# A post-LN decoder layer: who adds the output products behind the last heads, and the order of a top-k search

## The reference, cut to what matters

```python
x = ln(x + attn(x))           # 16 heads of 128; Wq, Wk, Wv, Wo are 4-bit codes times block scales
x = ln(x + xattn(x, ctx))     # ctx 2 x 1024 x 512
x = ln(x + ffn(x))            # silu(x Wg) * (x Wu), then Wd, 2048 inner features

def xattn(x, ctx):
    s = coef * (x @ Wqx.T) @ ctx.T                # [rows, 1024]
    s = s - max(s)
    thr = top_k(s, 54)[..., -1:]                  # the 54 largest of each row stay
    p = softmax(where(s < thr, -inf, s))
    return (p @ ctx) @ Wox.T
```

## Time and profile before

| | |
|---|---|
| Median of 3 runs | 959.24 us (959.2 to 959.57) |
| The profiled execution | 959.11 us, of which its span is 957.3 us |
| Busy, share of the span | TensorE 923.4 us (96%), VectorE 594.9 (62%), ScalarE 581.2 (61%), GpSimd 482.9 (50%) |
| The chain that ended last | TensorE 78%, VectorE 11%, ScalarE 5%, issue 4%, DMA 1% |
| Mean granted TensorE clock | 0.992 |

### The profile page before, as it was taken

How to read it: one execution, slowest core, us unless ns; L and a number is a source line. 1 busy time by engine, 2 the same in 40 slices (tenths; PEclk the granted TensorE clock), 3 DMA queues, 4 the chain that set the end, 5 groups by cost and what they waited for, 6 DMA issues and landing times.

```text
span 957.3 us, 13364 instructions
## 1 busy us (share of the span) xinstructions
PE 923.4 (96%) x4500; PEld 752.7 (79%) x4500; DVE 594.9 (62%) x1066; ACT 581.2 (61%) x1202; POOL 482.9 (50%) x377
## 2 busy tenths in 40 slices
PE   9999999999999999999999999799999899999997
PEld 7787778877788777877767787798878788888885
DVE  5666956578566676567585899984878214521114
ACT  4667876687766778687875456534655634443333
POOL 4256642646516366367664447543674751364440
PEclk9999999999999999999999999989999999999999
DMA  6531220122301222222122212332443241243331
GB/s 199 155 106 49 83 89 1 53 65 72 93 8 29 88 61 71 69 56 78 44 67 89 67 43 89 89 100 59 130 120 97 84 128 45 96 124 93 96 87 44
DMA packets 46103, 76.98 MB, mean 80 GB/s; under 512 B 5584, under 2 KB 11216, under 8 KB 45776
## 3 DMA queue, kind: packets, MB, share of 16 engines
q1 hardware_dynamic: 45600, 75.68, 27.0%
q10 hardware_dynamic: 432, 0.39, 0.1%
HBM read 73.69 MB, written 2.36 MB: 79 GB/s over the span
## 4 chain that ended last, share of the span: by engine, by line
PE 78%; DVE 11%; ACT 5%; issue 4%; DMA 1%; POOL 0%; SPq 0%; ACTq 0%; DVEq 0%; POOLq 0%
PE p L908 6%; PE p L909 6%; PE p L912 6%; PE p L681 5%; PE p L716 5%; PE p L683 4%; PE p L726 3%; PE p L703 3%; PE p L730 3%; PE p L727 3%; PE p L922 3%; PE p L924 3%; PE p L923 3%; PE p L663 2%; PE p L659 2%
## 5 line engine op out<-in xcount | busy, mean ns | idle before, releaser
L1517 DVE TENSOR_SCALAR_CACHE_REDUCE JK<-p,ssc 128x512 bf16<-128x512 f32 x112 | 83.8, 748 | 124.1 <-PE p L663 124.1
L2082 POOL TENSOR_TENSOR acc<-SX,acc 128x512 f32<-128x512 f32 x54 | 69.8, 1293 | 169.7 <-ACT SX L1075 141.9
L1999 POOL TENSOR_TENSOR V<-RAW,V 128x512 fp32r<-128x512 f32 x64 | 82.9, 1318 | 142.8 <-ACT V L1095 142.8
L1037 ACT ACTIVATE PR<-p,nms,ssc 128x512 f32<-128x512 f32 x112 | 87.2, 779 | 57.8 <-DVE JK L1517 56.8
L681 PE MATMUL p<-R 128*128 128x512 f32 x248 | 97.4, 393 | 1.0 <-DVE V L1510 0.8
L1999 POOL TENSOR_TENSOR C<-RAW,C 128x512 fp32r<-128x512 f32 x58 | 76.1, 1325 | 39.4 <-ACT C L1095 39.2
L1834 DVE TENSOR_TENSOR SX<-p,SX 128x512 f32<-128x512 f32 x32 | 22.1, 691 | 115.4 <-PE p L912 108.9
L1530 DVE TENSOR_TENSOR PT<-p,PT 128x512 fp32r<-128x512 f32 x128 | 87.4, 683 | 4.8 <-ACT PT L1060 4.7
L716 PE MATMUL p<-ident,PR 128*128 128x128 f32 x512 | 78.3, 275 | 0.5
L1060 ACT ACTIVATE PT<-p 128x512 fp32r<-128x512 f32 x128 | 75.7, 591 | 0.7 <-PE p L716 0.7
L683 PE MATMUL p<-R 128*128 128x512 f32 x192 | 75.1, 391 | 0.0
(11 more groups left out here) (246 smaller groups left out, 2711.7 us busy)
## 6 DMA issues: line engine op xcount, KB each, us to landing
RAW<-in_wg SPq DMA_DIRECT2D x32, 256.0 KB, 2.8
RAW<-in_wu SPq DMA_DIRECT2D x32, 256.0 KB, 2.7
RAW<-in_ctxn SPq DMA_DIRECT2D x32, 256.0 KB, 2.7
RAW<-in_wd SPq DMA_DIRECT2D x32, 256.0 KB, 2.7
RAW<-in_wq SPq DMA_DIRECT2D x19, 256.0 KB, 2.7
RAW<-in_wk SPq DMA_DIRECT2D x18, 256.0 KB, 2.7
RAW<-in_wv SPq DMA_DIRECT2D x16, 256.0 KB, 2.7
RAW<-in_wo SPq DMA_DIRECT2D x16, 256.0 KB, 4.7
```

Of the source, the lines that this page charges most:

```text
L1037: e.activation(PR[:, i % 2, :], P[i % 2][:, :], ACT.Exp, bias=nms[:, i % 4:i % 4 + 1], scale=ssc[:, 0:1] if HB[j][0] > 1 else SC, accum_ou ...
L1517: e.tensor_scalar(JK[:, :], P[i % 2][:, :], ssc[:, 1:2] if HB[i // 4][0] > 1 else -SC, None, ALU.mult, ALU.min, accum_out=nms[:, i % 4:i % ...
L1999: e.tensor_tensor(lo, RAW[:, slot[key], :], hi, ALU.subtract).then_inc(*c_lo.up(key))
```

## The change

- **Pairs 14 and 15 (and no longer VectorE).** `scaled_by_act` now also holds for n = 56 to 63; n = 54 and 55 stay with VectorE. From n = 54 on the scaled products go to CB and BO, not to SX0. GpSimd's addition becomes `add_scaled`; the four of pair 15 stand behind its loop, ahead of its low halves of `conv_ct(1, 4..7)`. On ScalarE the four `o_scale` of pair 15 alternate with those conversions, ahead of the table load for the square root.
- **The bias row** is made at i = 110 and added at i = 111 to 118, since CB and BO have to be free.
- **VectorE behind the loop**: one search step instead of three, the four first halves, the statistics of rows 4 to 7, then the reciprocal and application of rows 4 and 5, one step, those of rows 6 and 7, and three steps.
- **`alone`**: tiles 2 and 3 are ended by a new list that holds the rest of that tile only; `until` had alternated with tiles 3, 4 and 5.

```diff
+    def alone(self, n):
+        z = n % 2
+        assert self.live[z][0] == n
+        out = [(n, s) for s in range(self.live[z][1], 16)]
+        self.done.add(n)
+        self.live[z] = [n + 2, 0]
+        if n + 2 > 7:
+            del self.live[z]
+        return out
...
-        if i == 114:
+        if i == 110:
             take("borow")
...
-    return h == 1 and (q < 13 or q == 13 and tt < 2)
+    return h == 1 and not (q == 13 and tt >= 2)
...
+        def scaled_at(n):
+            return OBUF[:, n % 2] if n < 54 else (CB, BO)[n % 2][:, :]
...
 # ScalarE, behind the loop
-            for n in range(4, 8):
-                conv_ct(1, n)
-            search(topk.run(3))
+            for tt in range(4):
+                o_scale(NJ // 2 - 1, tt)
+                conv_ct(1, 4 + tt)
             act_table(ACT.Sqrt)
             ln_std(1, 4, 2)
+            search(topk.run(3))
+            ln_std(1, 6, 2)
             search(topk.run(1))
-            ln_std(1, 6, 2)
...
-            search(topk.until(2))
+            search(topk.alone(2))
             for hf in range(2):
                 px_high(2, hf, 6 + hf)
             conv_cn()
-            search(topk.until(3))
+            search(topk.alone(3))
             for hf in range(2):
                 px_high(3, hf, 6 + hf)
...
 # VectorE, behind the loop
             ot_low(NJ - 1)
-            search(topk.run(3))
+            search(topk.run(1))
             for tt in range(4):
                 o_add(NJ // 2 - 1, tt, 0)
-                o_add(NJ // 2 - 1, tt, 1)
-                if tt == 1:
-                    ln_stats(1, [4, 5], (15, 1))
-                    ln_rstd(1, 4, 2)
-                elif tt == 2:
-                    ln_apply(1, 4, 4)
-                    ln_apply(1, 5, 4)
+            ln_stats(1, [4, 5], (15, 1))
             ln_stats(1, [6, 7], (15, 1))
+            ln_rstd(1, 4, 2)
+            ln_apply(1, 4, 4)
+            ln_apply(1, 5, 4)
             search(topk.run(1))
             ln_rstd(1, 6, 2)
             ln_apply(1, 6, 6)
             ln_apply(1, 7, 6)
-            search(topk.run(1))
+            search(topk.run(3))
...
             cross_add(1, 5)
-            search(topk.until(2))
-            search(topk.until(3))
+            search(topk.alone(2))
+            search(topk.alone(3))
...
 # GpSimd
-                if 115 <= i <= 122:
-                    add_bias(i - 115, "bo2")
+                if 111 <= i <= 118:
+                    add_bias((4, 0, 1, 2, 3, 5, 6, 7)[i - 111], "bo2")
...
+            for tt in range(4):
+                add_scaled(NJ // 2 - 1, tt)
             for n in range(4, 8):
                 conv_ct(1, n)
```

More of the change, by code:

```diff
@@ L263, in row_writers @@
     out = ["bo1"] + [(q, h) for q in qs for h in range(2)]
-    if b == 0 and tt < 2:
-        out += [(12, 0), (12, 1), (13, 0), (13, 1), "bo2"]
-    elif b == 0:
+    if b == 0:
         out += [(12, 0), (12, 1), "bo2", (13, 0), (13, 1)]
@@ L1074, in o_scale @@
                     w.wait_ge(*masked_in[a].at())
-                e.activation(OBUF[:, n % 2], P[BANK["o", q, tt, 1]][:, :], ACT.Copy,
+                if n >= 54:
+                    w.wait_ge(*borowp.at())
+                    w.wait_ge(*rows[7].at("bo2"))
+                e.activation(scaled_at(n), P[BANK["o", q, tt, 1]][:, :], ACT.Copy,
                              scale=ri[:, 4 * (j % 4) + tt:4 * (j % 4) + tt + 1]).then_inc(*oscl.up((q, tt)))
@@ L1125, in conv_cn @@
                         w.wait_ge(*borowp.at())
-                        w.wait_ge(*rows[7].at("bo2"))
+                        w.wait_ge(*rows[7].at((15, 1)))
                     elif n < 5:
@@ L1995, in add_bias, with add_scaled @@
                 e.tensor_tensor(acc[:, r], acc[:, r], BO[:, :], ALU.add).then_inc(*rows[r].up(which))
+            def add_scaled(q, tt):
+                r = 4 * HB[2 * q][1] + tt
+                w.wait_ge(*oscl.at((q, tt)))
+                w.wait_ge(*rows[r].before((q, 1)))
+                e.tensor_tensor(acc[:, r], scaled_at(4 * q + tt), acc[:, r], ALU.add).then_inc(*rows[r].up((q, 1)))
             def conv(key, hi, lo):
@@ L2077, in gpsimd @@
                 if o_tile(i) and scaled_by_act(*o_tile(i), 1):
[L2078 to L2083, removed]
+                    add_scaled(*o_tile(i))
                 if i >= 2:
```

## The result

The changed kernel takes **969.1 us** (median of 4 runs, 968.1 to 970.5) where the kernel before, run beside it, takes 959.4 us: ratio 1.0106, 95% interval 1.0088 to 1.0124, so 9.7 us slower (10.2 by the ratio). The forecast was 966.7 us, with a range of 961.0 to 970.5. The profiled execution took 969.74 us, a span of 967.9 us, 10.6 more than that of before (957.3).

What follows compares the result with a forecast made beforehand. TensorE, busy nearly all the time, was taken as the bound, with VectorE's search deciding from 543 to 577 us. Terms +0.6 +1.4 +1.0 +0.7 +3.9 = +7.6 on 959.1 gave 966.7 us, range 961.0 to 970.5.

Steps and rivals of the forecast that it cites:

- bias row: Its product, ScalarE copy and GpSimd additions move four steps earlier: taken as 0 us, bounds -0.6 to +0.6.
- forecast A: Whole kernel, the prediction's main case: 964 to 970.5 us, chance 0.55.
- tile 3: Tiles listed alone, 612 to 623 us: exponential behind four copies and a conversion, +1.0 us, bounds +0.6 to +1.8.
- block 11: Feed-forward: tile 6's exponential comes late and holds its transposes and the output products; +3.9 us with clock, bounds +3.0 to +5.5.
- up to tile 0's exponential: Behind the last head: VectorE sheds additions but GpSimd holds applications; +0.6 us, bounds -2.0 to +1.3.
- half clock behind it: Behind the last head: TensorE's clock halves after idling some 3 us for the fourth query part; +1.4 us, bounds 0 to 2.6.
- blocks 5, 6: Feed-forward: one more exponential ahead of block 6's table load and activation; +0.7 us, bounds +0.6 to +1.2.
- GpSimd holds three of the four applications: VectorE behind the last head: first application free, other three slowed by GpSimd's work, 0.8 us each.
- GpSimd busy beside the mask: Tile 3's stage: GpSimd's work beside VectorE's mask raises the cost from +0.8 to +1.0 us.
- The place of the exponential: ScalarE at tile 3: exponential behind four copies and one conversion, so the product starts at 623.1 instead of 622.34; +0.8 us.
- The geometry: Block 11: output products that stood before TensorE's old wait now stand behind it; +3.4 us without the clock.
- Rival D: Feed-forward step lists keep their old place, so tile 6's transposes are not held: faster, 955.4 us, chance 0.06.

## Why the prediction was right, and where its sizes were off

Forecast +7.6 us, measured +9.7: forecast A, with every term's sign and place right, and a sum two us too small. The two us are mainly two sizes, the mask and half clock at tile 3 and the half clock in block 11.

| term | forecast | in the profile | by experiment |
|---|---|---|---|
| bias row | 0 | 0 | 0.0 at 484.97 |
| up to tile 0's exponential | +0.6 | +0.5 | 2.6 with the clock |
| half clock behind it | +1.4 | +1.1 | |
| tile 3 | +1.0 | +2.2 | 2.35, of it 1.02 the mask |
| blocks 5, 6 | +0.7 | +0.85 | 4.8 with block 11 |
| block 11 | +3.9 | +4.55 | 3.40 + 1.16 of clock |

**Behind the last head.** All steps came as forecast: the 1.93 us gone, an idle of 2.08 us for row 4, tile 0's exponential 0.5 us late, TensorE idle 3.53 us at the fourth query part. The choice on which the term hung, that GpSimd holds three of the four applications, was right: the four took 4.75 us, and 2.00 once GpSimd waits, so they were held for 2.75 us, where three held ones had been priced at some 2.5 from the earlier trace rows. That the first one slipped through was partly luck: with the wait filled, the same instructions took 5.88 us, all four held, and tile 0's exponential came 1.1 us later behind the score copy than in the changed kernel (31.23 and 30.10 us). The half clock behind it is the loose term: 1.1 us in the profile of the changed kernel, but 2.4 in that with joint lists (tile 2's transposes at 618.73, 3.4 late, against 0.95 at the fourth query part). No run takes it out by itself, so its size stays open within these two.

The SBUF — State Buffer page of the Trainium skill, section Who interferes with whom, says that the port pair is an exclusive lock for the length of an instruction, and that an instruction of VectorE with two SBUF inputs meets it when GpSimd reads SBUF. The traces agree in size: a mask that starts 0.03 us behind a conversion of 1.26 us takes 1.03 us more, and a MATCH_REPLACE8, with one such input, none. The applications, TENSOR_SCALAR with one such tensor, are held all the same, so the count of inputs alone does not tell who is.

**Tile 3 is the term that was mis-sized.** I put 0.2 us on "GpSimd busy beside the mask", although I had priced the same contention at 0.8 us for each application two paragraphs earlier. The mask took 2.31 us, 1.03 more. And I had put nothing on the clock there: TensorE's transposes came at half clock, so that from them to the product it took 2.59 us and not the 2.1 of the forecast. These two, 0.8 and 0.5 us above what I took, make up the 1.35 us by which the stage is over its forecast. The place of the exponential, behind four copies and a conversion, was forecast at 0.8; with the mask undisturbed 1.1 is left (8.07 - 6.99), of it 0.2 the clock.

**Blocks 5 and 6.** The mechanism as forecast: both exponentials in block 5's list, and the activation of block 6 at 703.20, 6.31 later than the earlier trace rows where TensorE was 5.3 late. Behind it tile 5's mask, too, took 2.39 us beside GpSimd, and the wait at its transposes is 1.76 us.

**Block 11.** The geometry was right (3.4 forecast, 3.40 measured); its clock was +1.16, not +0.5, and would have been +2.41 against an execution of the kernel before without half clock in this block. The reason given for it, three steps further back in every block, holds for tiles 4 and 5 only; for tiles 6 and 7 it is the lead that `until(3)` gave tile 4 by taking three of its steps along, and that tile 6 inherited. The list that I worked out gave the right slots for the exponentials all the same. Rival D, the step lists keeping their place, would have needed steps that the change doesn't add; the run that adds them, without the first half, came to 1.0041, so D's 955.4 had also missed the cost of the exponential's place at tile 3.

## What to carry to other kernels

A joint list of two tiles' steps does more than alternate: it fixes which tile leads, and which engine's queue meets the one step in sixteen that another engine does. Before listing a tile alone, work out in which slot each later hand-over step falls. Price each mask and each application of VectorE that stands on the path beside running GpSimd work at up to one GpSimd instruction more (1.03 us for a mask, 0.8 to 1 for an application here), and move the GpSimd work into its own waits: here that turned a loss of 2.6 us into a gain of 1.8. And steps that "cost nothing" on an engine cost what stands behind them in its queue.

## What the runs showed of the hardware

Two things I had not expected. The contention has the size of a turn-taking of whole instructions: 1.28 to 2.31 us for a mask with one conversion beside it, and back to 1.28 when the conversion waits; two applications 1.00, 1.96, 2.79 or 3.11 us. It goes the other way too: in the kernel before, a conversion that starts at 695.72, 0.63 us behind the start of a mask, takes 2.02 us instead of 1.3. That whole instructions take turns is read from these sizes, and no run tests it against a slowing down of both. And a TensorE that stands idle 2.35 us behind 4.09 us of idle transposes kept its full clock in block 11, where in the changed kernel the clock fell at 752.1, within the idle 6.37 us, and stayed at half until 758.9, a cost of 2.41 us; after 3.49 us idle it cost 1.6 us, and after 2.62 us 1.3 in two profiles and nothing in six; the filling itself cost nothing that can be seen, since the mask it waited for was the later one.
